# New instruction lists between two checks, dummy products on TensorE, and a weight ring of 19 places instead of 16

## The chip, the cores and the metric

One core of a Trainium2 chip. The time is that of one execution on the device, in microseconds (us), the median over several executions. PE is TensorE (DVE VectorE, ACT ScalarE, POOL GpSimd, SP the engine that issues most DMAs here). An instruction list is what one engine executes in order; engines meet only through semaphores.

## The reference, cut to what matters

```python
x = query                                             # 2 x 2048 x 256, float32
n = layernorm(x)
# 16 heads of 16; 32 learned patterns as keys and values
A = sparsemax(scale * (n @ Wq + bq) @ keys.T)         # per token and head over 32 patterns
x = x + layernorm((A @ values) @ Wo + bo)
n = layernorm(x)
# 16 slots attend to all tokens of a batch (softmax over the tokens)
o = slot_query + mha(slot_query, n, n)
# slot e goes through expert e of 16: 256 -> 1024 -> 256
h = layernorm(o) * g + b
o = o + (silu(h @ W1[e] + b1[e]) * silu(h @ Wg[e] + bg[e])) @ W2[e] + b2[e]
# every token attends to its batch's 16 slots, 16 heads
x = x + layernorm(mha(n, o, o))
```

Sparsemax needs, per token and head, a threshold tau such that max(z - tau, 0) adds up to 1.

## The kernel before

**Groups.** The 4096 tokens are worked on in 8 groups (NG) of 4 tiles of 128 tokens; groups 0 to 3 are batch 0, 4 to 7 batch 1. The residual stream x stays in SBUF (4 MB), as do the transposed second norms ynT (in `arena`, 4 MB): the slot scores read them once early, the last attention again at the end.

**Sparsemax, group i.** ACT normalizes (`norm_y`), PE transposes (`turn_y`) and makes scores into two PSUM banks (`scores_of`), ACT copies them to `scr` (`put_scores`), DVE takes the eight largest of each row of 32 with 16 MAX8 per tile (`sort_top`, L1551) and from their running sums a first tau (`threshold`). POOL subtracts it into `d` in two halves (`subtract`, L556), ACT clamps the halves at zero (`clamp`, L690), DVE marks and adds up (`count`, L1578 and L1579) and makes the final threshold `tauf` (`settle`, L1606). POOL takes it off the stored scores (`lower`, L548), and ACT's `signs` (L699) counts what is positive. After each batch a `check(b)` compares the two counts and, if a row needs it, repairs; it ends with the copy of a flag (L1652), which releases the batch's heads.

**Heads, tile n.** `turn_a` (4 transposes, L1019), `take_a` (ACT), `mix` with block-diagonal values that POOL makes (`values`, L539; semaphore bd_ready), `take_h`, `project` (L1038, L1040), `take_o` (ACT, L721). Then per group: `output_statistics` (DVE), `roots(1)` (POOL), `norm_o` (ACT, L662), `join` (DVE adds it to x, L1677, and takes statistics), `roots(2)`, `second_norm` (ACT), `turn_norm` (PE, L1066), `put_norm` (ACT, writes ynT), `slot_scores` (PE, L1075), `put_slot_scores`.

**The order between the checks.** While DVE does batch 1's sparsemax (groups 4 to 7), PE does batch 0's heads (groups 0 to 3) beside batch 1's scores. All four engines have these parts interleaved by lists written out by hand: on PE the `heads_of(g, steps)` calls with scores and norms between them, on ACT some 90 calls from `take_a(0)` on, on DVE and POOL the loops `for i in range(GB, NG)`. After the second check come batch 1's heads, and beside them the slot softmax and `to_slots` (short products in four steps for each batch, L1116 to L1136).

**Experts.** Weights are 48 loads of 1 MB (W1 and Wg of expert e, W2 of expert e-1, in turns). They go through a ring of R = 16 places of 8 KB per partition, in regions that are free by then (`slots_of`). SP's list issues load n with `fetch(n)`: the first 16 at written-out points between other waits, and from n = R on each when load n - R has been used (up_ps or down_ps). Per expert PE runs `grow` (two products of 512 columns for each of four column strips, L1306), `turn_up` (L1315), `sum_down` of the expert before (L1324) and `shrink` (L1336), with short DVE and ACT steps between. x lies in four of the places: `spill(g)` stores a finished group of x to the output tensor, `unused(j)` waits for two groups' stores and reads before a place of x is loaded, and `restore(j)` (L469) reads a group back when the last weights of its place have been used.

**Last attention.** Two small products each for keys and values (L1357), folds (L1365, L1371), and then per group `scores(j)` (L1388), softmax on DVE, ACT and POOL, `turn_prob` (L1399), `outputs` (L1412), a layernorm, the addition of x and the store.

Of the kernel before, what the change touches and what calls it, by code (L numbers as in the profile page):

```python
# [5 lines left out]
ALU = mybir.AluOpType  # L6
# [28 lines left out]
def build(nc, A, out):  # L35
    with ExitStack() as ctx:
# [3 lines left out]
        def sem(name):  # L40
# [7 lines left out]
        ynT = arena[:, 0:8192].rearrange("p (b c l) -> p b c l", b=NB, c=C)  # L48
# [11 lines left out]
        slots_of = ([home(xflat, 0), home(arena_late, 0), home(arena_late, 1), home(xflat, 1), home(scr1, 0), home(scr1, 1),  # L60
                     home(scr1, 2), home(xflat, 2), home(scr1, 3), heads[:, :], home(arena_late, 2), home(xflat, 3),
                     home(work, 2), home(work, 0), home(work, 1), home(work, 3)])
# [214 lines left out]
        back = [sem(f"back{q}") for q in range(2)]  # L277
        turned = sem("turned")
# [78 lines left out]
        def _(sp):  # L357
# [83 lines left out]
            sp.wait_ge(o_ps, 2 * KT)  # L441
            fetch(9)
# [3 lines left out]
            fetch(10)  # L446
            spill(7)
            unused(3)
            fetch(11)
            sp.wait_ge(g_ps, KT // 2 + KT // 4)  # L450
            fetch(12)
# [8 lines left out]
            def restore(j):  # L460
                if j >= 2:
                    sp.wait_ge(back[j % 2], 16 * (j // 2))
                last = max(n for n in range(3 * NE) if slots_of[n % R] is slots_of[(0, 3, 7, 11)[j // 2]])
                e, k = loads[last]
# [6 lines left out]
            for j in range(NG):  # L471
                restore(j)
# [10 lines left out]
        def _(pool):  # L483
# [96 lines left out]
            for i in range(GB, NG):  # L580
# [76 lines left out]
        def _(act):  # L657
# [28 lines left out]
            def clamp(i):  # L686
                for u in range(2):
# [48 lines left out]
            def put_norm(g):  # L736
                b, at = g // GB, (g % GB) * GT
                act.wait_ge(ynT_ps, g + 1)
                for c in range(C):
                    act.activation(ynT[:, b, c, at:at + GT], bT[c][:, :], ACT.Copy, bias=1.0).then_inc(ynT_sb, 1)  # L740
# [62 lines left out]
            take_a(1)  # L803
            take_h(0)
            clamp(4)
# [3 lines left out]
            put_scores(5, 1, range(2, 3))  # L809
            norm_y(6, tiles=range(2))  # L810
            put_scores(5, 1, range(3, TG))
            take_a(3)
            norm_y(6, tiles=range(2, TG))
# [4 lines left out]
            put_yT(6)  # L818
            take_o(3)
            put_scores(6, 1, range(1))  # L820
            signs(4, 1)
            put_scores(6, 1, range(1, 2))

            take_a(4)
            take_a(5)
            take_h(4)
            clamp(5)
            take_a(6)
            take_h(5)
            take_o(4)  # L830
            put_scores(6, 1, range(2, 3))
            norm_y(7, tiles=range(2))
            put_scores(6, 1, range(3, TG))
            take_a(7)
            take_h(6)
            take_o(5)
            norm_o(0)
            take_h(7)
            take_o(6)
            norm_y(7, tiles=range(2, TG))  # L840
            take_o(7)
            put_yT(7)
            second_norm(0)
            put_scores(7, 1, range(1))
            put_norm(0)
            signs(5, 1)
            put_scores(7, 1, range(1, 2))

            take_a(8)
            take_a(9)  # L850
            take_h(8)
            clamp(6)
            take_a(10)
            take_h(9)
            take_o(8)
            put_slot_scores(0)
            put_scores(7, 1, range(2, 3))
# [1176 lines left out]
```

## Time and profile before

| | us |
|---|---|
| median of 3 executions | 520.99 |
| lowest and highest | 520.46, 526.11 |
| the profiled execution's own time | 524.08 |
| its span, first to last instruction | 522.1 |
| PE busy (share) | 402.4 (77%) |
| DVE busy | 307.9 (59%) |
| ACT busy | 232.6 (45%) |
| POOL busy | 154.1 (30%) |

The profiled execution lasted 2.0 us more than its span. Times in rows are microseconds from the span's start. PEclk is the granted TensorE clock as a share of 2.4 GHz (0.5 is 1.2 GHz). Busy matmul times are modelled ends, so two may overlap; an f32 product is issued as two instructions.

### The profile page before, as it was taken

The page shows a single profiled execution, that of the slowest core. Times are in us where ns is not written, and L with a number is a line of the kernel's source. Part 1 is how long each engine was busy: PE and PEld are TensorE (multiplying, and loading weights), DVE is VectorE, ACT ScalarE, POOL GpSimd, SP SyncE. Part 2 cuts the span into 40 slices and gives each one's busy share as a digit, 9 for nine tenths or more (in the row PEclk, how much of TensorE's full clock was granted, in tenths as well). Part 3 has the DMA queues.
Part 4 walks back from the last instruction along what each step waited for, and adds up shares of the span by engine and source line. Part 5 has one row for each costly group of instructions (what it writes and reads, how often), then busy time and mean ns, then how long its engine had stood idle before and what let it go on. Part 6 is the DMA issues. An engine that isn't in the chain of part 4 may idle for free.

```text
span 522.1 us, 6829 instructions
## 1 busy us (share of the span) xinstructions
PE 402.4 (77%) x2023; PEld 251.6 (48%) x2023; DVE 307.9 (59%) x1176; ACT 232.6 (45%) x422; POOL 154.1 (30%) x253
## 2 busy tenths in 40 slices
PE   3868655869959583958999897599865669999981
PEld 3523222335434342534777666234322227888871
DVE  4699999978786837246522625323312213778994
ACT  2336765745848457547654744000000001237675
POOL 3115465656463452112320210100000000144454
PEclk9997788769989879879999999779989895999996
DMA  5291101101010315245322571579999996201223
GB/s 153 88 332 48 30 12 41 40 1 41 1 41 1 96 56 201 75 146 177 122 81 82 171 272 26 216 266 401 388 398 393 391 374 210 81 1 40 72 85 126
DMA packets 42301, 75.38 MB, mean 144 GB/s; under 512 B 1686, under 2 KB 36124, under 8 KB 38172
## 3 DMA queue, kind: packets, MB, share of 16 engines
q1 hardware_dynamic: 41208, 73.76, 40.3%
q10 hardware_dynamic: 1060, 1.22, 0.8%
q8 instruction: 16, 0.26, 0.2%
q14 instruction: 17, 0.14, 0.1%
HBM read 66.58 MB, written 8.39 MB: 144 GB/s over the span
## 4 chain that ended last, share of the span: by engine, by line
PE 52%; DVE 19%; ACT 8%; DMA 5%; SPq 5%; issue 5%; POOL 4%; DVEq 1%; POOLq 0%; ACTq 0%
PE bank L1075 6%; PE bank L1412 5%; PE bank L1388 5%; SPq L396 5%; PE bank L1104 4%; PE bank L1306 4%; PE bank L1040 4%; DVE top L1551 4%; PE bank L1007 3%; PE bank L1029 3%; DMA arena<-in_L_ffn_e_W_dram 3%; PE bank L1019 2%; DVE stats L1476 2%; DMA work<-in_L_ffn_e_Wg_dram 2%; PE bank L1066 2%
## 5 line engine op out<-in xcount | busy, mean ns | idle before, releaser
L1007 PE MATMUL bank<-Wz,yT 128*128 128x512 f32 x128 | 71.9, 714 | 26.0 <-DVE top L1551 23.4
L1007 PEld LDWEIGHTS bank<-Wz,yT 128*128 128x128 f32 x128 | 28.7, 233 | 61.7 <-issue 49.9
L1551 DVE MAX8 top<-bank 128x8 f32<-128x32 f32 x512 | 51.7, 178 | 6.7 <-ACT scr L683 3.9
L941 ACT ACTIVATE d<-d 128x32 f32<-128x32 f32 x16 | 3.7, 229 | 104.6 <-DVE d L1897 104.6
L526 POOL TENSOR_SCALAR veps<-mv 128x4 f32<-128x4 f32 x24 | 6.7, 278 | 119.4 <-DVE mv L1479 88.8
L1040 PE MATMUL bank<-aWo,hoT 128*128 128x256 f32 x128 | 37.0, 413 | 3.5 <-DVE arena L1665 3.5
L631 POOL TENSOR_TENSOR work<-work 128x512 f32<-128x512 f32 x16 | 16.6, 1060 | 70.1 <-DVE work L1962 70.1
L662 ACT ACTIVATE arena<-arena,shift,rstd 128x256 f32<-128x256 f32 x64 | 33.5, 596 | 2.6 <-POOL shift L646 2.6
L1075 PE MATMUL bank<-arena,Wd 128*128 128x512 f32 x64 | 32.1, 647 | 1.2 <-ACT arena L740 1.2
L1665 DVE TENSOR_TENSOR arena<-bank,Wz 128x256 f32<-128x256 f32 x16 | 6.7, 418 | 43.8 <-PE bank L1040 43.8
L1886 DVE TENSOR_TENSOR d<-bank,slotT 128x4 f32 (+1 forms) x16 | 2.6, 165 | 50.0 <-PE bank L1324 50.0
L1104 PE MATMUL bank<-d,work 128*128 128x256 f32 x128 | 30.2, 381 | 0.5 <-ACT d L768 0.5
L1412 PE MATMUL bank<-scr,work 128*128 128x256 f32 x128 | 29.1, 381 | 1.6 <-ACT work L954 1.6
L1388 PE MATMUL bank<-scr,arena 128*128 128x256 f32 x128 | 29.0, 381 | 0.0
L1040 PEld LDWEIGHTS bank<-aWo,hoT 128*128 128x128 f32 x128 | 22.4, 194 | 13.7 <-issue 9.9
L1029 PE MATMUL bank<-heads 128*64 128x256 f32 x128 | 22.3, 427 | 6.1 <-ACT hoT L713 4.5
L1412 PEld LDWEIGHTS bank<-scr,work 128*128 128x128 f32 x128 | 24.2, 190 | 5.3 <-ACT work L954 2.1
L529 POOL TENSOR_TENSOR rstd<-veps,mhalf 128x4 f32<-128x4 f32 x24 | 26.0, 1083 | 2.0
L707 ACT ACTIVATE heads<-bank 128x512 f32<-128x512 f32 x32 | 18.6, 593 | 17.6 <-PE bank L1019 17.6
L1388 PEld LDWEIGHTS bank<-scr,arena 128*128 128x128 f32 x128 | 24.0, 192 | 3.3 <-DVE work L1949 0.2
L1104 PEld LDWEIGHTS bank<-d,work 128*128 128x128 f32 x128 | 24.1, 196 | 3.0 <-ACT d L768 1.0
L1306 PE MATMUL bank<-x,top 128*32 128x512 f32 x64 | 20.2, 764 | 6.2 <-DMA scr<-in_L_ffn_e_Wg_dram 3.5
(255 smaller groups left out, 872.9 us busy)
## 6 DMA issues: line engine op xcount, KB each, us to landing
x<-in_L_ffn_e_W_dram SPq DMA_DIRECT2D x9, 1024.0 KB, 10.9
scr<-in_L_ffn_e_W_dram SPq DMA_DIRECT2D x8, 1024.0 KB, 13.3
work<-in_L_ffn_e_W_dram SPq DMA_DIRECT2D x8, 1024.0 KB, 14.6
arena<-in_L_ffn_e_W_dram SPq DMA_DIRECT2D x5, 1024.0 KB, 7.6
xin<-in_L_attn_query_dram SPq DMA_DIRECT2D x8, 512.0 KB, 4.1
x<-in_L_attn_query_dram SPq DMA_DIRECT2D x1, 4096.0 KB, 16.6
out_dram<-x SPq DMA_DIRECT2D x8, 512.0 KB, 3.4
arena<-in_L_ffn_e_Wg_dram SPq DMA_DIRECT2D x4, 1024.0 KB, 10.4
```

The costliest lines, as they stand in the source:

```text
L396: sp.dma_start(dst, src).then_inc(e_in[n % R], 16)
L529: pool.tensor_tensor(rstd[:, k, :], veps[:, k, :], mhalf[:, :], ALU.pow).then_inc(root[k], 1)
L662: return act.activation(dst, src, ACT.Identity, bias=shift[:, k, t:t + 1], scale=rstd[:, k, t:t + 1])
L1007: mm = pe.matmul(bZ[t % 2][:, :], yT[:, c, t * P:(t + 1) * P], Wz[:, c, :], start=(c == 0), stop=(c == C - 1))
L1029: mm = pe.matmul(psH[64 * a:64 * a + 64, :], bdh[:, n % TG, :], quarter[:, :, a, :], start=True, stop=True)
L1040: mm = pe.matmul(psO, hoT[:, n % 2, m, :], aWo[:, m, :], start=(m == 0 and n >= KT), stop=(m == 1))
L1075: mm = pe.matmul(bT[m][:, :], Wd[:, c, m * P:(m + 1) * P], ynT[:, b, c, gb * GT:(gb + 1) * GT], start=(c == 0), stop=(c == C - 1))
L1104: mm = pe.matmul((bZ[0] if n < 8 else bank[7])[:, c * 2 * P:(c + 1) * 2 * P], yn[:, kt, c::C], pT[:, n % 2, u * 2 * P:(u + 1) * 2 * P], st ...
L1306: mm = pe.matmul(bank[q][32 * k:32 * k + 32, :], hcol[:, q, c, :], pair[g][:, c * FF + half * 512:c * FF + (half + 1) * 512], start=(c == ...
L1388: mm = pe.matmul(ps, ynT[:, b, c, at:at + P], Wc[:, b, c, :], start=(c == 0), stop=(c == C - 1))
L1412: mm = pe.matmul(ps, cpT[:, u, (v * 2 + m) * P:(v * 2 + m + 1) * P], Vc[:, b, m, :], start=(m == 0), stop=(m == 1))
L1551: mx = v.max(top[:, h * TG + t, :], bZ[t % 2][:, h * NS:(h + 1) * NS])
```

## The change

The diff has four parts.

1. *Lists between the checks.* ACT's calls from `take_a(0)` to `take_o(15)` are in a new order: clamps are split in halves with copies of heads between them, `norm_o(g)` stands whole and early, `signs` of groups 5 and 6 stand later. PE's `heads_of` pieces are cut elsewhere; the first scores of group 7 stand before `turn_norm(0)`, `turn_norm(1)` and `slot_scores(1)` go inside the heads of group 3. POOL makes the next group's first values between `roots(1)` and `roots(2)`. On DVE `count` adds up first and marks after; for group 7 it adds up in two halves, each behind one half of the clamp; `group_maximum(0)` goes behind `threshold`.
2. *Dummy products* (`keep_clock(bank, times)`): each is one bf16 product of 128 x 128 with 512 columns from the constant `chain` into a bank that nobody reads. Nine before `turn_p(12)`; 5, 4, 3, 15 and 4 before and behind the steps of `to_slots(1, ...)`; 4, 3 and 2 around the last expert's `shrink` and `sum_down`.
3. *Norms to DRAM.* ynT is laid out by group. `send_away(g)` stores groups 2 to 7 (0.5 MB each) after `put_norm(g)`, `left(k)` waits for a pair's stores and slot scores, and `fetch_back(k)` reads a pair back after the last weights of its place. `scores(j)` waits for it from group 2 on.
4. *A ring of 19 places*: the three regions of these pairs are places 5, 10 and 15. The early fetches are 19, in the same written-out places of SP's list, and refills start with load 19.

```diff
+            def send_away(g):
+                k = g // 2 - 1
+                sp.wait_ge(ynT_sb, 2 * (g + 1))
+                sp.dma_start(away[k, :, (g % 2) * 1024:(g % 2 + 1) * 1024], arena[:, 1024 * g:1024 * (g + 1)])\
+                    .then_inc(gone[k], 16)
+
+            def left(k):
+                sp.wait_ge(gone[k], 32)
+                sp.wait_ge(s_ps, 2 * (2 * k + 4))
...
             fetch(4)
+            send_away(2)
+            send_away(3)
+            left(0)
+            fetch(5)
             sp.wait_ge(a_ps, KT + 8)
-            fetch(5)
+            fetch(6)
             spill(4)
             sp.wait_ge(a_ps, KT + 12)
-            fetch(6)
+            fetch(7)
+            send_away(4)
             spill(5)
             unused(2)
-            fetch(7)
+            fetch(8)
+            send_away(5)
             sp.wait_ge(a_ps, 2 * KT)
-            fetch(8)
+            fetch(9)
+            left(1)
+            fetch(10)
...
+            fetch(14)
+            send_away(7)
+            left(2)
+            fetch(15)
             sp.wait_ge(pT_ps, KT)
-            fetch(13)
-            fetch(14)
+            fetch(16)
+            fetch(17)
             sp.wait_ge(g_ps, KT)
-            fetch(15)
+            fetch(18)
...
+            fetch_back(0)
+            restore(0)
+            restore(1)
+            fetch_back(1)
+            restore(2)
+            restore(3)
+            fetch_back(2)
+            for j in range(4, NG):
                 restore(j)
```

PE's list, and POOL's and DVE's loops:

```diff
-            heads_of(1, range(3, TG + 2))
+            heads_of(1, range(3, 4))
             turn_y(7)
+            heads_of(1, range(4, TG + 2))
+
+            heads_of(2, range(2))
+            scores_of(7, range(2))
             turn_norm(0)
-            scores_of(7, range(2))
+            heads_of(2, range(2, 3))
             slot_scores(0)
-
-            heads_of(2, range(3))
             scores_of(7, range(2, TG))
             heads_of(2, range(3, TG + 2))
+
+            heads_of(3, range(3))
             turn_norm(1)
+            heads_of(3, range(3, 4))
             slot_scores(1)
-
-            heads_of(3)
+            heads_of(3, range(4, TG + 2))
...
                     roots(1, g - 1)
+                if i < NG - 1:
+                    values(g + 1, range(2))
+                if g > 0:
                     roots(2, g - 1)
                 if i < NG - 1:
                     lower(i, 1)
-                    values(g + 1, range(2))
...
+                if last:
+                    for u in range(2):
+                        v.wait_ge(relued, i * 2 + (u + 1))
+                        v.tensor_reduce(exc[:, u * HR // 2:(u + 1) * HR // 2], d3[:, u * NH // 2:(u + 1) * NH // 2, :, :],
+                                        AX_X, ALU.add).then_inc(newton, 1)
+                else:
+                    v.wait_ge(relued, i * 2 + 2)
+                    v.tensor_reduce(exc[:, :], d3, AX_X, ALU.add).then_inc(newton, 1)
```

ACT's list, the part of groups 5 and 6 (new order):

```python
            clamp(5, range(1))
            take_o(3)
            take_a(4)
            clamp(5, range(1, 2))
            take_a(5)
            take_h(4)
            take_a(6)
            take_h(5)
            norm_y(7, tiles=range(2))
            take_o(4)
            norm_o(0)
            put_scores(6, 1, range(2, TG))
            take_a(7)
            norm_y(7, tiles=range(2, TG))
            ...
            take_o(12)

            signs(6, 1)
            take_a(15)
            take_h(14)
            take_o(13)
            clamp(7)
            mark(7)
            put_slot_scores(1)
            norm_o(2)
            take_h(15)
            take_o(14)
            take_o(15)
            signs(7, 1)
```

The dummy products:

```diff
+            def keep_clock(bk, times):
+
+                idle = chain[:, :, :].rearrange("p r k -> p (r k)")
+                for _ in range(times):
+                    pe.matmul(bank[bk][:, :], idle[:, 0:P], idle, start=True, stop=True)
...
             pe.wait_ge(dve_part, PREP + MS)
-            for step in range(4):
+            pe.wait_ge(hbias, 1)
+            for step, times in enumerate((5, 4, 3, 15)):
+                keep_clock(1, times)
                 to_slots(1, step)
+            keep_clock(1, 4)
...
+                if e == NE - 1:
+                    keep_clock(1, 4)
                 shrink(e)
+            keep_clock(1, 3)
             sum_down(NE - 1)
+            keep_clock(1, 2)
```

## Rows read from the trace of the kernel before

**Rows 1.** Windows by stage: length; busy time (instructions) by engine; PEclk, DMA share, GB/s

```profile
108.37:209.94 101.57, 76.70 (x296) 42.30 (x296) 74.83 (x317) 63.88 (x119) 50.09 (x59) 0.87 0.16 56
209.94:327.20 117.26, 104.49 (x514) 74.55 (x514) 49.44 (x153) 65.38 (x126) 21.14 (x55) 0.96 0.39 131
341.26:427.03 85.77, 62.69 (x560) 26.68 (x561) 23.09 (x72) 3.44 (x15) 2.46 (x13) 0.93 1.02 382
427.03:445.06 18.03, 16.86 (x93) 11.90 (x93) 5.63 (x21) 1.51 (x2) 0.00 (x0) 0.53 0.76 239
445.06:520.50 75.44, 64.91 (x333) 56.76 (x331) 59.96 (x139) 42.31 (x81) 33.03 (x52) 0.95 0.19 63
120.00:150.00 30.00, 24.27 (x112) 13.98 (x110) 24.20 (x120) 21.32 (x44) 16.60 (x20) 1.00 0.11 36
```

**Rows 2.** The page's slices of 13 us, DMA busy in tenths

```profile
DMA  5291101101010315245322571579999996201223
```

**Rows 3.** Groups by line, 108 to 210: busy us, mean ns, idle before

```profile
L1007 PE MATMUL bank<-Wz,yT 128*128 128x512 f32 x40 | 19.9, 644 | 0.0
L1551 DVE MAX8 top<-bank 128x8 f32<-128x32 f32 x192 | 19.5, 178 | 5.0 <-ACT scr L683 3.9 <-issue 1.1
...
L1579 DVE TENSOR_REDUCE exc<-d 128x64 f32<-128x2048 f32 x4 | 9.1, 2278 | 8.1 <-ACT d L690 8.1
...
L699 ACT ACTIVATE above<-scr,tiny 128x2048 bf16<-128x2048 f32 x4 | 8.0, 2000 | 0.0
```

**Rows 4.** Timeline of ACT, norm_o of group 0

```profile
142.05 2.06 ACT L662 ACTIVATE arena<-arena,shift,rstd 128x256 f32<-128x256 f32 x4
```

**Rows 5.** Timeline of POOL, subtraction of group 7

```profile
184.48 3.78 POOL L556 TENSOR_TENSOR d<-scr,tau 128x1024 f32<-128x1024 f32 x2 [0.71 <-DVE tau L1565]
```

**Rows 6.** Timeline of DVE, between the checks: start, duration, instruction, idle before

```profile
144.14 1.23 DVE L1677 TENSOR_TENSOR x<-x,arena 128x1024 f32<-128x1024 f32 x1 [3.08 <-ACT arena L662]
...
177.22 0.23 DVE L1606 TENSOR_TENSOR tauf<-tau,rcnt 128x64 f32<-128x64 f32 x1
...
194.21 2.29 DVE L1579 TENSOR_REDUCE exc<-d 128x64 f32<-128x2048 f32 x1 [8.14 <-ACT d L690]
...
209.94 0.15 DVE L1652 COPY flag<-moved 128x1 f32<-128x1 f32 x1 [2.66 <-issue]
```

**Rows 7.** Timeline of PE, turn_norm(0) and slot_scores(1)

```profile
151.55 1.89 PE L1066 MATMUL bank<-ident,work 128*128 128x128 f32 x8 [4.50 <-ACT work L662]
...
183.47 6.60 PE L1075 MATMUL bank<-arena,Wd 128*128 128x512 f32 x8 [1.18 <-ACT arena L740]
```

**Rows 8.** Timeline of SP's queue: loads 13 and 14, first refill, restores

```profile
323.74 1.00 SPq L396 DMA_DIRECT2D work<-in_L_ffn_e_W_dram  x2
...
341.26 0.38 SPq L396 DMA_DIRECT2D x<-in_L_ffn_e_W_dram  x1
...
422.78 21.85 SPq L469 DMA_DIRECT2D x<-out_dram  x8
```

**Rows 9.** The chain that ended last: start, us, what

```profile
337.57 3.67 PE bank L1306 x16
...
352.25 1.85 PE bank L1306 x16
...
415.73 11.17 DMA work<-in_L_ffn_e_Wg_dram
...
438.10 3.59 PE bank L1357 x16
```

**Rows 10.** Timeline of PE: a bf16 product, and three waits

```profile
126.17 0.26 PE L1038 MATMUL bank<-ab,ones 3*128 3x256 bf16 x1 [0.57 <-ACT arena L721]
...
317.02 1.09 PE L1090 MATMUL bank<-ident,work 128*128 128x128 f32 x8 [2.50 <-ACT work L756]
...
336.10 0.29 PE L1135 MATMUL bank<-ident,yT 16*128 16x16 f32 x1 [3.52 <-DVE yT L1775]
...
434.27 1.93 PE L1336 MATMUL bank<-work,xin 128*32 128x256 f32 x16 [0.28 <-issue]
```

More of the change, by code:

```diff
@@ L277, in build @@
         back = [sem(f"back{q}") for q in range(2)]
+        gone = [sem(f"gone{k}") for k in range(NG // 2 - 1)]
+        home_again = [sem(f"home_again{k}") for k in range(NG // 2 - 1)]
         turned = sem("turned")
@@ L445, in _, with emptied @@
             sp.wait_ge(x_new, NG)
-            fetch(10)
+            fetch(12)
+            send_away(6)
             spill(7)
             unused(3)
-            fetch(11)
+            fetch(13)
             sp.wait_ge(g_ps, KT // 2 + KT // 4)
-            fetch(12)
+            fetch(14)
+            send_away(7)
+            left(2)
+            fetch(15)
             sp.wait_ge(pT_ps, KT)
-            fetch(13)
-            fetch(14)
+            fetch(16)
+            fetch(17)
             sp.wait_ge(g_ps, KT)
-            fetch(15)
+            fetch(18)
             for n in range(R, 3 * NE):
                 fetch(n)
[L460 to L464, printed above, removed]
+            def emptied(place):
+                e, k = loads[max(n for n in range(3 * NE) if n % R == place)]
                 if k < 2:
@@ L468, in restore, with fetch_back @@
                     sp.wait_ge(down_ps, e + 1)
-                sp.dma_start(x[:, j * TG:(j + 1) * TG, :], ot[:, j * TG:(j + 1) * TG, :]).then_inc(back[j % 2], 16)
-            for j in range(NG):
+            def fetch_back(k):
+                emptied(places_y[k])
+                sp.dma_start(arena[:, 2048 * (k + 1):2048 * (k + 2)], away[k, :, :]).then_inc(home_again[k], 16)
+            def restore(j):
+                if j >= 2:
+                    sp.wait_ge(back[j % 2], 16 * (j // 2))
+                emptied(places_x[j // 2])
+                sp.dma_start(x[:, j * TG:(j + 1) * TG, :], ot[:, j * TG:(j + 1) * TG, :]).then_inc(back[j % 2], 16)
+            fetch_back(0)
[6 more added lines that the diff above has]
+            for j in range(4, NG):
                 restore(j)
@@ L684, in put_scores, with clamp @@
                                    bZ[t % 2][:, :].rearrange("p (h s) -> p h s", h=NH), ACT.Copy).then_inc(z_sb, 1)
-            def clamp(i):
-                for u in range(2):
+            def clamp(i, halves=range(2)):
+                for u in halves:
                     half = slice(u * 1024, (u + 1) * 1024)
@@ L803, in _ @@
             take_a(1)
+            clamp(4, range(1))
             take_h(0)
-            clamp(4)
+            clamp(4, range(1, 2))
             take_a(2)
@@ L861, in _ @@
             take_o(9)
-            norm_o(1, range(2, TG))
-            put_scores(7, 1, range(3, TG))
             take_h(11)
             take_o(10)
+            take_a(12)
             take_o(11)
-            second_norm(1)
-            put_norm(1)
-            signs(6, 1)
-            take_a(12)
             take_a(13)
             take_h(12)
-            clamp(7)
-            mark(7)
+            second_norm(1)
             take_a(14)
             take_h(13)
+            put_norm(1)
             take_o(12)
-            put_slot_scores(1)
-            norm_o(2, range(2))
+            signs(6, 1)
             take_a(15)
@@ L883, in _ @@
             take_o(13)
-            norm_o(2, range(2, TG))
+            clamp(7)
+            mark(7)
+            put_slot_scores(1)
+            norm_o(2)
             take_h(15)
@@ L1571, in steps_ahead, with count @@
                 return i * NW if b == 0 else GB * NW + (i - GB) * (NW + 1)
-            def count(i, b, marks):
-                v.wait_ge(relued, i * 2 + 2)
-                if not marks:
-                    v.wait_ge(signed, i)
-                    v.tensor_scalar(above[:, :], d[:, :], 0.0, None, ALU.is_gt).then_inc(newton, 1)
-                v.tensor_reduce(exc[:, :], d3, AX_X, ALU.add).then_inc(newton, 1)
+            def count(i, b, marks, last=False):
+                if last:
[6 more added lines that the diff above has]
+                    v.tensor_reduce(exc[:, :], d3, AX_X, ALU.add).then_inc(newton, 1)
                 if marks:
@@ L1591, in settle @@
             def settle(i, b, marks, last=False):
-                at = steps_ahead(i, b) + (2 if marks else 3)
+                at = steps_ahead(i, b) + (2 if marks and not last else 3)
                 v.wait_ge(newton, at)
@@ L1817, in _ @@
                     output_statistics(g - 1)
-                count(i, 1, i == NG - 1)
+                count(i, 1, i == NG - 1, last=i == NG - 1)
                 if 0 < g < 3:
```

79 lines of the change are left out of this document (40 added, 39 removed).

## The prediction

> **What bounds the kernel now.** I read the windows by stage first [rows 1]. The reader is to see that no one engine carries the whole span. Between the two checks (108.37 to 209.94) PE is busy 76.7 of 101.6 us, DVE 74.8, ACT 63.9: nobody is full, so the stage is a chain that goes round the engines. From 209.94 to 327.2 PE has 104.5 of 117.3 us. In the experts (341.26 to 427.03) the DMA share is 1.02 at 382 GB/s while PE has 62.7 of 85.8: loads bound it. From 445 on PE is the bound again until the last tiles. The page's slice row of DMA [rows 2] shows the same plateau of nines, nine slices long, and next to nothing in most slices ahead of it. So a gain must come from the chain between the checks, from fewer loads left when the experts start, or from PE's clock in the 32 us around the experts, where the grants are low (0.53 in the row of 427.03 to 445.06).
>
> **Between the checks.** I walked the four instruction lists of the new kernel, with this stage's durations: 16 MAX8 per tile 1.6 us (0.178 us each, overlapping a little), one big sum 2.28, one tile of scores on PE 1.7, a sign pass 2.0 plus 0.1 [rows 3], four scaled tiles on ACT 2.06 [rows 4], a subtraction 3.78 in two halves [rows 5]; an instruction starts when its engine is free and its releaser has been done for 0.05 to 0.25 us, as in the trace.
> - Group 4: nothing differs until ACT's clamp. ACT clamps the first half before it copies heads, and DVE adds up before it marks, so tauf comes at 120.3 instead of 120.7.
> - Group 5: the signs of group 4 no longer part the first two score copies of group 6, and take_o(3) stands behind half a clamp. DVE's output statistics end at 133.7 (before: 135.8), POOL's roots at 135.9 (138.9). Now norm_o(0) stands right behind take_o(4), so ACT runs it from 136.0 to 138.1; before, it stood behind a projection that waits for four score products, and ran from 142.05 [rows 4]. DVE idled 3.08 us on it and joined at 144.14 [rows 6]. In the new order DVE finishes its count at 139.0 and joins at once. tauf: 143.5 instead of 148.7, 5.2 earlier.
> - Group 6: PE stood 4.50 us before turn_norm(0), with the scores of group 7 behind it, and the clock fell in the wait (its 8 transposes took 1.89 us) [rows 7]. In the new order the scores of group 7 go first: tiles at 148.7 and 150.4. The output statistics end at 155.0 (163.7), the clamp at 157.8 (165.5), the count at 163.0, norm_o(1) at 160.7, the join at 166.1. tauf: 167.6 instead of 177.4 [rows 6], 9.8 earlier.
> - Group 7: group_maximum(0), 1.2 us, goes behind the threshold. Threshold at 173.9, subtraction done at 178.0 instead of 188.26 [rows 5]: 10.2 earlier.
> - The end: mix(14) needs the values that POOL makes only after that subtraction, and ACT's clamp(7) now stands behind take_h(14) and take_o(13). PE idles some 7 us before it, so I let it run at half clock there, as it did at 183.5 (slot scores 6.60 us [rows 7]). Clamp done at 183.5, mark 185.4, count 187.4, tauf 189, DVE's lowering 191.2, join 194.3 (norm_o(2) at 190.1), signs(7) 194.5, and the check's own 3.8: settled at 199.5 instead of 209.94. Before, the count had idled 8.14 us on the clamp [rows 6], 6 us after the subtraction's end; it is 5.5 in the walk, so this tail gains next to nothing.
>
> I take 10.5 us off. Bounds: 13 off if PE keeps its full clock at the end (slot scores 3.4 instead of 6.6); 4 off if each of the steps that I let run tightly loses 2 us, which is what the seen waits vary by. After the check the same lists run as before, so the later stages only move. POOL's reordered values(g+1) ahead of roots(2) cost nothing: their h_ps is long there.
>
> **Six groups' norms away, ring of 19.** Added: six stores of 0.5 MB between 214 and 312 us, three loads of 1 MB back, and four waits for PE and DMA on SP's queue. What is queued behind these waits on SP are the fetches and the spills, each of which was already held by something near: left(0) lets fetch(5) go at 238 (s_ps of group 3), left(1) at 283, left(2) at 313; send_away(4) holds spill(5) 6 us, and unused(2) behind it came at 269 anyway. The last early loads still go at 323.7 and 327.2 [rows 8] with little in flight before, land by 334, and so all 19 places are full before the first refill. The DMA is at 131 GB/s in that stage [rows 1], so 6 MB more hide. Price without that cover: 0.5 MB at 382 GB/s is 1.4 us each.
> Then the experts. The first refill is issued at 341.26 [rows 8], when grow(0) is done; PE waits for Wg of expert 15, load 45, until 426.9 [rows 9]. With 16 places these are loads 16 to 45, 30 of them in 85.7 us; 2 us are the first one's way, so 2.79 each (1.05 MB at 382 GB/s: 2.74). With 19 places three fewer: 8.4 us. PE could go faster: grow steps stand 4.2 us apart where it has its weights, so 15 experts after the first need 63 us of the 77 that are left; the bound stays DMA. Bounds: 8.2 to 8.6 if all three are in; none if they come late.
> Read-backs: restore(0) is issued at 422.78, behind the last weights [rows 8]; now 1 MB stands before it and 2 MB between the restores. 7 MB from about there at 260 to 390 GB/s are 18 to 27 us. Group 2's norm, first in the queue, lands before 440 where PE wants it at 455 (this trace's times), groups 4 and 6 have 15 us more each. Cost 0; if the cover went, 2.7 us for each MB.
>
> **Dummy products.** One is a bf16 product of 512 columns. The trace has only 256 bf16 columns (0.26 us [rows 10], the next product 0.21 later) and f32 instructions of 512 columns (16 in 1.85 at full clock, four beside each other in the array, so 0.46 for each four [rows 9]). So it lies between 0.21 and 0.46; I take 0.22, because an f32 product is issued as two instructions for the same columns and bf16 as one, and 0.43 at half clock.
> - Nine before turn_p(12): 2.0 us in a wait of 2.50 [rows 10]. Clock there is 1.00 already. 0.
> - 5, 4, 3, 15 and 4 in the slot steps of batch 1: 6.8 us in gaps of 1.0, 0.7, 0.5, 3.5 [rows 10] and 0.8. The overhang is 0.6. They keep the clock: grow(0) took 3.67 us at half and takes 1.85 at full [rows 9], the small transposes 0.3 less. The refill starts at grow(0)'s end, and DMA bounds from there, so the gain goes through once: net 1.5 off. Bounds: 2 off, and 6.8 lost if a dummy takes 0.43 and more.
> - 4, 3 and 2 around the last expert: PE waits there 0.28 [rows 10], 0.54 and 0.35 us, 3.9 us of dummies at half clock, so 2.7 lost. If they lift the clock at once, shrink(15), sum_down, L1357 (3.59 for 16 [rows 9]) and what follows halve: 3.8 gained against 0.8 lost, 3.1 off. I take 0, near the middle.
>
> What the row of the tail shows: PE is busy 16.9 of 18.0 us at a granted 0.53 [rows 1], that is 1.2 GHz most of the time although it hardly rests; it ran instructions of 512, 2, 256 and 32 columns there, and the clock is back at 445 after three groups of 128 and 256. The Trainium skill (TensorE: Matmul & The Clock Gate, Part 1: The HAM clock gate) says that the slow clock is the default and that sustained activity of the engine releases it. By it alone the tail ought to have been fast already, and a few wide products more should make it so: the tail term would be -3.1 instead of 0. This trace does not agree, by 17 us of that row; the rule stays as a rival below.
>
> **The sum.** The profiled execution took 524.08 us, its span 522.1, 2.0 lie around it. -10.5 -8.4 -1.5 + 0 = -20.4: 503.7 for an execution like that one. The median shown is 520.99, 3.1 below it; the same terms on the median give 500.6.
>
> **Rivals.**
> - *The chain between the checks loses its slack.* PE falls to half clock at each wait, not only the last, and norm_o, join and clamp slip 2 us three times: 4.5 off instead of 10.5, 506.6. For it: the clock fell at both norm waits before [rows 7]. Against it: it was 1.00 from 120 to 150 [rows 1], and the new order has fewer waits until the last group.
> - *The wide dummies lift the clock in the tail.* 3.1 off more, and the stage between the checks at its better end by 1: 496.5. Worked out: shrink(15) 0.9, sum_down 0.4, L1357's first half 0.9 and what hangs on it 1.6, less 0.8 of dummies. For it: the clock did come back at 445 once the products were back to back. Against: in the row of 427.03 to 445.06 the engine was nearly as busy, and it did not.
> - *The ring gives nothing.* The three more loads are held on SP (left(2) or a spill late) and still outstanding at 341: 8.4 fewer, 509.0. Against: the three loads issued from 323.7 on take 10 us, so 7 us lie between their landing and the first refill.
> - *Slower: the clock of the whole stage.* PE's products between the checks are 76.7 us at 0.87, or 66.7 us of full clock; the rest of the stage, 24.9, is not PE's. If the new order makes PE's work arrive in pieces, at mean clock c the stage takes 66.7/c + 24.9. It eats the other terms' 10 us at c = 0.77 and makes the kernel 1% slower at 0.73; at 0.70 the stage takes 120 us, 18.6 more, and the kernel 529.7. Against it: the 1.00 above, and less idle PE to pull it down.
>
> **How the numbers follow.** Forecast 0.50; chain without slack 0.22; clock lifted in the tail 0.17; ring nothing 0.07; slower 0.04. The forecast's own range is 497 to 504. For 8 in 10, the first two rivals belong in it with their spread: 494.5 to 508.5, which leaves out the ring's case and the slow one and some of each edge. A change of 1% (5.2 us) is about what a measurement tells from none. All cases but the last are faster by more than 1% (0.96, and I give 0.95); the last is split: 0.03 within 1%, 0.02 slower.
>
> **What would show it.** In the profile after: the second flag near 199.5 and the subtraction of group 7 ending near 178; DVE's idle before its join of group 0 gone; experts from first refill to the wait for Wg of expert 15 in 77 us instead of 85.7, DMA share still 1.0; first grow in 1.9 us; norms back before PE asks, so no wait of L1388 on DMA. It is wrong if PE's waits in the experts vanish (then PE bounds and 8.4 is too much), if a wait for the norms opens a gap between 445 and 500, or if the stage's PE clock is under 0.85.

## The result, and the profile after

The changed kernel takes 499.23 us (median of 4, 496.82 to 501.44), the kernel before 523.55 beside it (median of 4, 520.46 to 527.11). The ratio is 0.9586, interval 0.954 to 0.9632: 4.1% faster, where 3.9% was forecast and 500.6 us. The medians lie 24.3 us apart. The profiled execution took 501.44, its span is 499.4, so 22.7 us less span than before; the stages below are read from this one execution of each kernel.

The windows by stage of the changed kernel, cut at the same events as [rows 1] (flag to flag, flag to first `grow`, first refill to the wait for Wg of expert 15, from there to the first score of the last attention, and the rest):

```profile
109.44:202.16 92.72, 72.63 (x296) 40.44 (x296) 75.64 (x317) 63.22 (x118) 45.18 (x59) 0.88 0.17 62
202.16:331.25 129.09, 118.10 (x579) 81.51 (x579) 53.96 (x169) 66.09 (x128) 22.44 (x61) 0.95 0.55 187
333.23:409.77 76.54, 62.75 (x560) 26.90 (x561) 23.20 (x72) 3.44 (x15) 2.46 (x13) 0.91 1.02 384
409.77:422.39 12.62, 12.04 (x101) 7.29 (x101) 5.18 (x20) 1.51 (x2) 0.00 (x0) 1.00 1.04 365
422.39:498.00 75.61, 64.87 (x333) 56.72 (x332) 60.32 (x141) 42.31 (x81) 33.04 (x52) 0.97 0.32 106
```

The reader is to see four things. The first row has almost the same busy times as before in 8.85 us less. The third has the same DMA share in 9.2 us less. The fourth has a granted clock of 1.00 where it was 0.53. The last carries three more megabytes of read-backs and is as long as before: from the first score to the end of the span it is 77.01 us, before 77.04, and no score product there waited for a DMA.

| stage, us | before | after | difference | term in the sum |
|---|---|---|---|---|
| start to first flag | 108.37 | 109.44 | +1.07 | 0 |
| flag to flag | 101.57 | 92.72 | -8.85 | -10.5 |
| second flag to first grow | 127.63 | 129.09 | +1.46 | +0.3 |
| first grow to first refill | 3.69 | 1.98 | -1.71 | -1.8 |
| refill to wait for load 45 | 85.77 | 76.54 | -9.23 | -8.4 |
| that wait to first score | 18.03 | 12.62 | -5.41 | 0 |
| first score to end | 77.04 | 77.01 | -0.03 | 0 |

The critical chain shows where the new bounds lie. DMA has 4% of it (before 5%), and the dummies (L1189) now stand in it, each four in 0.86 to 0.97 us:

```profile
322.79 0.86 PE bank L1189 x4
...
330.35 0.97 PE bank L1189 x4
331.32 1.90 PE bank L1358 x16
```

The first `grow` takes 1.90 us; its answer in [rows 9] took 3.67.

### The profile page after: what moved, and what is told of

It is laid out like the page before. It is cut to its first block, busy times and chain, and to the rows that moved or that the text cites. A ratio compares the mean times of both kernels' runs of the same rounds, so it can differ in the third digit from the quotient of the medians.

```text
span 499.4 us, 6939 instructions
## 1 busy us (share of the span) xinstructions
PE 403.0 (81%) x2072; PEld 249.7 (50%) x2072; DVE 308.8 (62%) x1177; ACT 232.0 (46%) x422; POOL 149.2 (30%) x253
## 4 chain that ended last, share of the span: by engine, by line
PE 53%; DVE 20%; ACT 8%; issue 5%; SPq 5%; DMA 4%; POOL 3%; DVEq 1%; POOLq 0%; ACTq 0%
PE bank L1469 6%; PE bank L1445 6%; PE bank L1112 5%; PE bank L1078 5%; PE bank L1141 5%; PE bank L1045 4%; DVE top L1608 4%; SPq L403 4%; PE bank L1358 4%; DMA x<-in_L_ffn_e_W_dram 3%; PE bank L1067 3%; DVE exc L1639 2%; DVE stats L1533 2%; PE bank L1057 2%; PE bank L1388 2%
## 5 line engine op out<-in xcount | busy, mean ns | idle before, releaser
L1045 PE MATMUL bank<-Wz,yT 128*128 128x512 f32 x128 | 70.7, 704 | 24.2 <-DVE top L1608 21.6
L1078 PE MATMUL bank<-aWo,hoT 128*128 128x256 f32 x128 | 39.4, 434 | 3.5 <-DVE arena L1727 3.5
L568 POOL TENSOR_SCALAR veps<-mv 128x4 f32<-128x4 f32 x24 | 5.7, 237 | 110.4 <-DVE mv L1536 83.3
L1078 PEld LDWEIGHTS bank<-aWo,hoT 128*128 128x128 f32 x128 | 23.7, 205 | 14.1 <-issue 10.2
L1112 PE MATMUL bank<-arena,Wd 128*128 128x512 f32 x64 | 29.9, 610 | 0.0
L571 POOL TENSOR_TENSOR rstd<-veps,mhalf 128x4 f32<-128x4 f32 x24 | 24.9, 1039 | 2.0
L1358 PE MATMUL bank<-x,top 128*32 128x512 f32 x56 | 17.1, 742 | 7.0 <-DMA arena<-in_L_ffn_e_Wg_dram 3.6
## 6 DMA issues: line engine op xcount, KB each, us to landing
arena<-in_L_ffn_e_W_dram SPq DMA_DIRECT2D x9, 1024.0 KB, 13.8
```

Of the source, the lines that this page charges most:

```text
L571: pool.tensor_tensor(rstd[:, k, :], veps[:, k, :], mhalf[:, :], ALU.pow).then_inc(root[k], 1)
L1045: mm = pe.matmul(bZ[t % 2][:, :], yT[:, c, t * P:(t + 1) * P], Wz[:, c, :], start=(c == 0), stop=(c == C - 1))
L1078: mm = pe.matmul(psO, hoT[:, n % 2, m, :], aWo[:, m, :], start=(m == 0 and n >= KT), stop=(m == 1))
L1112: mm = pe.matmul(bT[m][:, :], Wd[:, c, m * P:(m + 1) * P], ynT[:, g, c, :], start=(c == 0), stop=(c == C - 1))
L1358: mm = pe.matmul(bank[q][32 * k:32 * k + 32, :], hcol[:, q, c, :], pair[g][:, c * FF + half * 512:c * FF + (half + 1) * 512], start=(c == ...
```

## The experiments

Four executions each, compared with the kernel before on the same chip. The stages are read from the profile of one of them, as in the table above; all numbers are us, "changed" is the changed kernel, "experts" is from the first refill to PE's wait for load 45, and "tail" from there to the first score of the last attention. The kernel before had medians of 523.55, 521.35, 521.04 and 522.45 in four measurements, the changed kernel 499.23 and 498.36. So the stages carry the argument and the medians confirm it, and differences of 1 or 2 us in a median say little.

| run | median | flag to flag | flag to grow | to refill | experts | tail |
|---|---|---|---|---|---|---|
| before | 523.55 | 101.57 | 127.63 | 3.69 | 85.77 | 18.03 |
| changed | 499.23 | 92.72 | 129.09 | 1.98 | 76.54 | 12.62 |
| e1 lists only | 511.85 | 90.23 | 128.27 | 3.69 | 85.65 | 15.22 |
| e2 ring only | 514.06 | 101.56 | 132.84 | 3.46 | 76.25 | 15.36 |
| e3 dummies only | 517.75 | 101.76 | 129.85 | 1.99 | 84.05 | 12.60 |
| e4 no dummies | 502.82 | 90.23 | 128.07 | 3.70 | 77.46 | 15.48 |
| e5 no tail dummies | 502.22 | 90.60 | 128.20 | 1.98 | 76.54 | 14.91 |
| e6 values first | 494.70 | 85.62 | 129.38 | 1.98 | 76.02 | 12.61 |
| e7 dummies at the check | 498.68 | 90.87 | 127.93 | 1.99 | 76.25 | 13.48 |
| e8 both | 490.93 | 86.78 | 126.74 | 1.98 | 76.85 | 12.58 |
| e9 changed again | 498.36 | 92.72 | 129.06 | 1.98 | 75.93 | 12.60 |
| e10 no head dummies | 505.12 | 92.73 | 128.95 | 3.69 | 77.39 | 13.75 |
| e11 no ring | 508.40 | 92.74 | 129.10 | 1.99 | 84.37 | 12.61 |

### e1: the lists alone

The kernel before with the new lists of ACT, PE, POOL and DVE; nothing else of the diff.

> The kernel before with the new lists alone (16 places, no dummy products, norms stay). My theory: the parts add up, each in its own stage. The stage between the two checks takes 92 to 94 us instead of 101.6 and everything behind it only moves, so the time is 8 to 10 us under the kernel before (ratio 0.981 to 0.985). Rival: PE's half clock in the first slot scores after the second check gives part of it back in a part of the profiles; then 6 to 7 us.

Measured: 511.85 us (508.87 to 514.29), ratio 0.9815 (0.974 to 0.9891). Flag to flag is 90.23. The lists give 11.3 us in this stage (7.6 to 9.6 expected) and hand on all of it but 0.6. My theory held; the rival's half clock behind the second flag is there, but it was there before too. The tail is 2.8 us shorter although nothing in it was touched. PE entered it at full clock in both profiles: before, the clock fell 1 to 2 us later, here only in the group of 32-column products, 8 us in.

### e2: the ring alone

The parts 3 and 4 of the diff (spill, read-back, 19 places), old lists, no dummies.

> The kernel before with the norms' spill and the ring of 19 alone. My theory: loads bound the experts, so from the first refill to the wait for Wg of expert 15 it takes 76.5 to 77.4 us instead of 85.8, and the rest stays as it was: 8 to 9.5 us under the kernel before (ratio 0.982 to 0.985). Rival for the tail: if the 5.4 us that the changed kernel gained between that wait and the first score of the last attention come from where the last wait falls and not from the dummies, the tail is 12.6 us long here too and the gain is 13 to 14 us; if the dummies make it, the tail stays 18.

Measured: 514.06 us (511.34 to 517.95), ratio 0.9866 (0.9783 to 0.9949). The experts take 76.25, as my theory wants. Neither expectation for the tail held: it is 15.36, between both. And 5.2 us were lost between the second flag and the experts, which I had not expected. PE's timeline shows 3.1 of them; the first two lines stand where the changed kernel has its nine dummies:

```profile
318.73 1.97 PE L1130 MATMUL bank<-ident,work 128*128 128x128 f32 x8 [2.50 <-ACT work L797]
320.53 3.78 PE L1144 MATMUL bank<-d,work 128*128 128x256 f32 x8
...
335.54 1.89 PE L1171 MATMUL bank<-d,hT 128*16 128x256 f32 x4 [0.47 <-DVE hT L1801]
```

The same eight transposes took 1.09 us before, behind the same wait of 2.50 [rows 10], and the product behind them 2.00:

```profile
318.37 2.00 PE L1104 MATMUL bank<-d,work 128*128 128x256 f32 x8 [0.25 <-ACT d L768]
```

The two groups end 2.2 us later for it, and the last line's half clock (1.89 us, before 1.04) costs 0.9. The other 2.1 lie ahead of the wait: behind the second flag the clock came back later than in the profile before. The clock can fall in this wait or not: it fell here, and not in the kernel before, in e1 and in e4, each with the same wait of 2.50.

### e3 and e4: the dummies alone, and none of them

```diff
 e3: the kernel before, plus every keep_clock(...) of the diff
 e4: the changed kernel, less every keep_clock(...)
```

> The kernel before with the dummy products alone. My theory: grow(0) starts at full clock and takes 1.9 us instead of 3.7 (net 2 us earlier for the first refill), and the tail shortens from 18 to 13 us only if the dummies are its cause: 7 us under the kernel before in all (ratio 0.986). Rival (the tail is luck of the last wait): 2 us in all (ratio 0.996), tail 17 to 18.

> The changed kernel without any dummy product. My theory: lists and ring keep 18 us, 2 are lost at the head of the experts; whether the tail is 18 us again (505 to 507 in all) or stays near 13 (501 to 502) tells whether the dummies or the place of the last wait made the tail short.

Measured: e3 517.75 us (515.74 to 519.58), ratio 0.993 (0.9861 to 1.0); e4 502.82 us (502.41 to 503.88), ratio 0.9648 (0.9584 to 0.9712). The tail is 12.60 with the dummies and 15.48 without, so both theories were half right: 2.9 us come from the dummies, and the other 2.5 of the 5.4 from where the clock happened to fall in the profile before (the part on the tail, below, compares them). e3's median is 3.6 us under the kernel before, half of my 7, while the two profiled spans differ by 6.8. In its profile 2.1 us are lost behind the second flag, ahead of the first dummy, where its program is the kernel before's, and e2 lost the same 2.1 there: that is not the edit. What else parts the median from the profile stays open.

### e5: no dummies in the tail

```diff
-                if e == NE - 1:
-                    keep_clock(1, 4)
                 shrink(e)
-            keep_clock(1, 3)
             sum_down(NE - 1)
-            keep_clock(1, 2)
```

> The changed kernel without the nine dummy products around the last expert; the 31 in the slot steps and the nine before them stay. If these nine make the short tail (my theory after the first four runs), the stretch from the wait for Wg of expert 15 to the first score of the last attention takes 15.2 to 15.5 us where PE enters it at full clock and 18 where not, and grow(0) still takes 1.9 us. Rival: the 2.9 us between the runs with and without dummies come from the head's dummies too (a clock that stayed up); then the tail stays 12.6.

Measured: 502.22 us (500.7 to 507.78), ratio 0.97 (0.96 to 0.9799). The tail is 14.91, and `grow(0)` still short: the nine make it. PE's timeline of e5, last expert on:

```profile
413.17 1.07 PE L1388 MATMUL bank<-scr,xin 128*32 128x256 f32 x16 [0.62 <-DMA scr<-in_L_ffn_e_W_dram]
414.78 0.63 PE L1376 MATMUL bank<-sel,y 128*128 128x2 f32 x4 [0.55 <-DVE y L1939]
415.76 1.45 PE L1409 MATMUL bank<-d,Wz 128*128 128x32 f32 x8 [0.35 <-DVE d L1944]
417.03 1.89 PE L1409 MATMUL bank<-d,hoT 128*128 128x32 f32 x8
418.74 2.05 PE L1417 MATMUL bank<-d,above 128*128 128x128 f32 x8
420.58 1.91 PE L1423 MATMUL bank<-aWo,d 128*128 128x256 f32 x4
```

and of the changed kernel:

```profile
415.77 1.07 PE L1388 MATMUL bank<-scr,xin 128*32 128x256 f32 x16
416.77 0.82 PE L1189 MATMUL bank<-chain 128*128 128x512 bf16 x3
417.43 0.59 PE L1376 MATMUL bank<-sel,y 128*128 128x2 f32 x4
417.88 0.59 PE L1189 MATMUL bank<-chain 128*128 128x512 bf16 x2
418.37 1.05 PE L1413 MATMUL bank<-d,Wz 128*128 128x32 f32 x8
419.26 1.06 PE L1413 MATMUL bank<-d,hoT 128*128 128x32 f32 x8
420.45 1.16 PE L1421 MATMUL bank<-d,above 128*128 128x128 f32 x8
421.45 1.03 PE L1427 MATMUL bank<-aWo,d 128*128 128x256 f32 x4
```

Both enter at full clock. Without the dummies it falls within the first group of 32-column products (1.45 us, then 1.89 for the same eight); with them the last three groups run in little more than half the time. The dummies did not lift a fallen clock, they kept a full one. They did two things at once, they filled PE's gaps and they put wide products between narrow ones; which of the two kept the clock, no run separates.

### e6: values first

```diff
+                if g == 3:
+                    values(g, range(2, TG))
                 subtract(i, 1)
-                if g > 0:
+                if 0 < g < 3:
                     values(g, range(2, TG))
```

> The changed kernel with POOL making the second pair of values of group 3 before the last subtraction instead of after it. In the changed kernel PE stands 5.84 us before mix(14) on these values, and ACT's last clamp stands behind it. My theory: that couples the clamp to PE, so the clamp's halves come 5 to 6 us earlier and the stage between the checks is 4 to 6 us shorter (87 to 88.5 us). Rival: the chain then waits for the output norm of group 2 and the lowered signs, which gives only 1 to 2 us.

Measured: 494.7 us (493.63 to 495.17), ratio 0.9529 (0.948 to 0.9578). Flag to flag is 85.62, 7.1 less than in the changed kernel's profile and better than I had expected. Of these, 5.0 are the swap: from the subtraction's end to the flag it is 15.5 us, in the changed kernel, e1 and e4 20.5. The other 2.1 lie ahead of the subtraction, where a wait of PE differed (see the part on the stage between the checks). The median is 3.7 us under e9's and 4.5 under the changed kernel's. PE's timeline of the changed kernel, with the wait, and DVE's, with its idle time for the clamp:

```profile
175.60 0.60 PE L1057 MATMUL bank<-ident,arena 128*128 128x128 f32 x4
182.04 1.12 PE L1067 MATMUL bank<-heads 128*64 128x256 f32 x4 [5.84 <-issue]
183.09 0.39 PE L1076 MATMUL bank<-ab,ones 3*128 3x256 bf16 x1
183.41 2.08 PE L1078 MATMUL bank<-aWo,hoT 128*128 128x256 f32 x4
185.28 4.38 PE L1112 MATMUL bank<-arena,Wd 128*128 128x512 f32 x8
```

```profile
186.88 2.35 DVE L1635 TENSOR_REDUCE exc<-d 128x32 f32<-128x1024 f32 x2 [6.21 <-ACT d L734]
```

and the same places of e6:

```profile
173.95 0.65 PE L1069 MATMUL bank<-heads 128*64 128x256 f32 x4 [0.29 <-issue]
...
175.93 3.60 PE L1114 MATMUL bank<-arena,Wd 128*128 128x512 f32 x8
```

```profile
178.62 1.22 DVE L1637 TENSOR_REDUCE exc<-d 128x32 f32<-128x1024 f32 x1 [0.49 <-ACT d L736]
180.26 1.22 DVE L1637 TENSOR_REDUCE exc<-d 128x32 f32<-128x1024 f32 x1 [0.42 <-ACT d L736]
```

PE's wait is gone and with it the half clock behind it, and DVE's idle time before the last sums falls from 6.21 to 0.9. The trace puts PE's wait down to "issue"; the run shows that it was POOL's values, queued behind a subtraction that needs group 7's threshold. POOL's timeline, of the changed kernel and of e6, has the two in either order:

```profile
177.91 3.78 POOL L598 TENSOR_TENSOR d<-scr,tau 128x1024 f32<-128x1024 f32 x2 [2.67 <-DVE tau L1622]
181.65 0.55 POOL L581 TENSOR_TENSOR heads<-vrep,jmask 128x64 f32<-128x64 f32 x2
```

```profile
172.65 2.00 POOL L581 TENSOR_TENSOR heads<-vrep,jmask 128x64 f32<-128x64 f32 x2
175.36 3.78 POOL L598 TENSOR_TENSOR d<-scr,tau 128x1024 f32<-128x1024 f32 x2 [0.71 <-DVE tau L1624]
```

The values took 0.55 us behind the subtraction, and PE began at 182.04.

### e7 and e8: dummies in the wait for the check

```diff
+            pe.wait_ge(a_sb, KT)
+            keep_clock(4, 26)
             for n in range(KT, 2 * KT + 2):
                 heads_step(n, KT, 2 * KT)
```

> The changed kernel with 26 dummy products more, on PE before the heads of batch 1, in its wait for the second check (6.8 us idle in the profile, half clock behind it until about 209). If the clock bounds the first heads of batch 1, from the second flag to grow(0) it takes 1.5 to 3 us less than 129.1; rival: the wait for psO, the norms and the statistics bounds there and nothing changes.

> Values first and the 26 dummies together. If both hold as expected, the stage between the checks is 87 to 88.5 us, what follows 1.5 to 3 us shorter, and the whole 6 to 8 us under the changed kernel. If PE then still idles before the second check, the dummies are still hidden; if not, they add up to 5.7 us and the gain is lost.

Measured: e7 498.68 us (496.89 to 499.34), ratio 0.9591 (0.9538 to 0.9645), not to be told from the changed kernel. Flag to `grow` is 127.93, 1.2 less than in the changed kernel's profile but only 0.3 less than in e5's, so e7 alone decides nothing; its dummies ended 1.1 us after the flag. e8, with e6's edit too: 490.93 us (489.7 to 493.15), ratio 0.9445 (0.9396 to 0.9495), 126.74 us from flag to `grow`, 2.4 less than the changed kernel and 2.6 less than e6. It is the best of all: its slowest execution is under e6's fastest (493.63). In e8 the 26 dummies ran while DVE was at the check, and the heads behind it ran at full clock:

```profile
189.41 6.89 PE L1191 MATMUL bank<-chain 128*128 128x512 bf16 x26
196.28 0.66 PE L1059 MATMUL bank<-ident,scr 128*128 128x128 f32 x4
196.77 1.18 PE L1106 MATMUL bank<-ident,work 128*128 128x128 f32 x8
```

In the changed kernel the two groups behind the dummies took 1.12 and 1.91 us. The dummies end 0.2 us after the flag at 196.07, so a few less would do.

### e9 to e11: the changed kernel again, no head dummies, no ring

```diff
 e10:
-            for step, times in enumerate((5, 4, 3, 15)):
-                keep_clock(1, times)
+            for step in range(4):
                 to_slots(1, step)
-            keep_clock(1, 4)
 e11: the changed kernel with the 16 places and the loads of the kernel before, norms not spilled
```

> The changed kernel itself once more, as the measure for the two runs beside it and for how far its stages vary between profiles. Theory: 497 to 501; between the checks 90 to 93 us, from the second flag to grow(0) 127.5 to 130, experts 76 to 77.5, tail 12.6 to 13.5; what varies is where the half clock falls, not the work.

> The changed kernel without the 31 dummies in the slot steps (the nine before turn_p(12) and the nine of the tail stay). Theory: grow(0) at half clock, 3.7 us to the first refill instead of 2.0, about 0.3 us earlier start: 1.5 to 2 us slower than the changed kernel. If the refill's start did not bound the experts, no difference.

> The changed kernel with 16 places and the norms kept in SBUF; lists and all dummies as changed. Theory: experts 84 to 86 us from the first refill to the wait for Wg of expert 15, everything else as in the changed kernel: 8 to 9.5 us slower. Rival: the spilled norms cost something before or after (DMA beside the heads, read-backs beside the last attention), then the other stages are shorter here.

Measured: e9 498.36 us (497.2 to 501.24), e10 505.12 us (502.32 to 505.59), e11 508.4 us (504.59 to 509.81). Against e9, e11 loses 10.0 us in the median and 8.4 in the experts, and every other stage is within 0.2: the spill and the read-backs cost nothing. The rival fell. e10 loses 6.8 us in the median where I expected 1.5 to 2, and 4.0 in the profile: 1.7 to the refill, 1.5 in the experts, 1.2 in the tail. The tail's part is not shown to be the head dummies' work: PE entered it at half clock (its last `grow` took 3.56 us), and so it did in e7, which has them all (3.31 us, tail 13.48). SP's timeline of e10 shows where the experts' part comes from:

```profile
335.05 0.38 SPq L403 DMA_DIRECT2D x<-in_L_ffn_e_W_dram  x1
...
340.65 0.33 SPq L403 DMA_DIRECT2D arena<-in_L_ffn_e_Wg_dram  x1
```

and the same of e9:

```profile
333.69 0.38 SPq L403 DMA_DIRECT2D x<-in_L_ffn_e_W_dram  x1
...
337.12 0.33 SPq L403 DMA_DIRECT2D arena<-in_L_ffn_e_Wg_dram  x1
```

At half clock `grow(1)` is late too, and the third refill comes 5.6 us after the first instead of 3.4. By the prediction's 2.74 us for each, the first two refills are 5.5 us of DMA work, an estimate by which the queue ran nearly dry. The 2.8 us between the median's loss and the profile's are the choice of the execution: e9's profile is of its slowest, 501.24, which is 2.9 over its median, e10's (505.13) of its median one. e4, without a single dummy, has a median of 502.82, under e10's; so 6.8 us is not the price of the 31.

## Why the prediction was right, point by point

**Between the checks: right in mechanism, one step too hopeful.** The walk's milestones count from the first flag. tauf of group 5: 35.1 forecast, 34.5 measured; the join of group 0 follows its count with no idle time, as written. tauf of group 6: 59.2 forecast, 61.3 measured. The failing step is "tiles at 148.7 and 150.4" for the scores of group 7. PE's timeline of the changed kernel:

```profile
128.21 1.04 PE L1057 MATMUL bank<-ident,arena 128*128 128x128 f32 x8
131.80 0.75 PE L1067 MATMUL bank<-heads 128*64 128x256 f32 x4 [2.55 <-ACT heads L751]
...
135.14 2.08 PE L1078 MATMUL bank<-aWo,hoT 128*128 128x256 f32 x4
137.00 4.62 PE L1045 MATMUL bank<-Wz,yT 128*128 128x512 f32 x8
```

take_a(4) stands behind half a clamp and take_o(3), PE waited 2.55 us for it, and the clock fell for the next 7 us (a projection of 2.08 us against 1.13 at full clock). The scores came 2.4 us later than walked. In e1 and e4 the same lists take 90.23, under the 91.1 walked; e1's PE timeline at the same place:

```profile
130.67 0.65 PE L1026 MATMUL bank<-heads 128*64 128x256 f32 x4 [1.44 <-ACT heads L709]
...
134.39 3.60 PE L1004 MATMUL bank<-Wz,yT 128*128 128x512 f32 x8
```

In e1 the granted clock from 134 to 142 was 1.00 (in e4 from 132 to 140 too), in the changed kernel's profile 0.68. What goes with it is the wait: 2.55 or 2.56 us in the four profiles that took 92.7 (the changed kernel, e9, e10, e11), 0.25 to 1.53 in the four that took 90.2 to 90.9 (e1, e4, e5, e7). Why PE comes to this place earlier in some executions stays open. So -10.5 lies between the two ways that this stage runs, -8.9 and -11.3. The rival "the chain loses its slack" was the right mechanism at a fraction of its size.

**The end of this stage** was forecast to gain next to nothing because mix(14) waits for values behind the subtraction: subtraction's end to flag 21.5 us forecast, 20.5 measured, 21.7 before. e6 shows that this wait was worth 5.0 us (15.5). The prediction named the wait and left it.

**Ring: right.** 8.4 us forecast. The four profiles with 16 places take 85.77, 85.65, 84.05 and 84.37 us in the experts, mean 84.96; the nine with 19 places 75.93 to 77.46, mean 76.58: 8.4. Against e9, e11 shows 8.4 as well. DMA share stayed 1.02. Spill and read-back at nothing: shown by e11 and by the last stage, 76.9 to 77.4 in every run. One reading of the prediction was off without harm: DMA's row of slices [rows 2] has six nines in its plateau, not nine slices.

**Head dummies: right in what they do, and too low.** 0.22 us each was right (nine in 2.1 us), and grow(0) gave its 1.7. In the profile the refill comes only 0.25 us sooner after the second flag, because slot_scores(3), long before any dummy, is already 1.3 us late against the flag (half clock behind the check). The step that was too low is "the gain goes through once". In four profiles without head dummies (before, e1, e4, e10) the third refill came 5.5 to 5.6 us after the first; these are the longest in the experts of their kind, 85.77 and 85.65 with 16 places, 77.46 and 77.39 with 19. In the other nine it came 3.4 us after, and the experts took 84.05 and 84.37, or 75.93 to 76.85. So the dummies give another 1.1 to 1.5 us in the experts, and of the 9.2 there the ring's part is 7.9 to 8.4. e2 is among the nine though it has no dummies: its clock came back inside grow(0).

**Tail: wrong, by its clock.** "I take 0, near the middle" measured -5.4, outside my bound of -3.1. The step had priced the dummies at half clock, since the tail of the kernel before ran so by its mean of 0.53. That mean hid where the clock fell. PE came to the tail of the kernel before at full clock and lost it inside the last `grow`:

```profile
426.00:428.00 2.00, 0.97 (x12) 0.45 (x16) 0.00 (x0) 0.00 (x0) 0.00 (x0) 1.00 1.09 347
428.00:430.00 2.00, 2.00 (x15) 0.63 (x6) 0.00 (x0) 0.00 (x0) 0.00 (x0) 0.57 1.10 347
```

The last `grow` of the kernel before, of e2 and of e4:

```profile
427.03 2.45 PE L1306 MATMUL bank<-work,top 128*32 128x512 f32 x16 [3.54 <-DMA work<-in_L_ffn_e_Wg_dram]
...
422.13 1.92 PE L1346 MATMUL bank<-scr,top 128*32 128x512 f32 x16 [3.42 <-DMA scr<-in_L_ffn_e_Wg_dram]
...
407.50 3.35 PE L1347 MATMUL bank<-scr,top 128*32 128x512 f32 x16 [1.21 <-DMA scr<-in_L_ffn_e_Wg_dram]
```

e2 waited nearly as long and kept its clock until the 32-column products. e4 entered at half clock and had it back at the end of this `grow`, and so had e7 and e10. The four other profiles without dummies in the tail (e1, e2, e4, e5) all lost the clock at the 32-column products and took 14.9 to 15.5 us, so the 18.03 of before was an unlucky draw worth some 2.5 us, and the dummies' part is 2.3 to 2.9. The eight profiles with them never lost it: 12.6 us, and 13.5 and 13.8 where they entered at half clock. The rival with the lifted clock (3.1; its own terms add up to 3.0) had nearly the size of the dummies' part, for the wrong reason: where the dummies ran, the clock was already full, and they kept it. The Trainium skill says (TensorE: Matmul & The Clock Gate, Part 1: The HAM clock gate) that sustained activity releases the slow clock. e4, e7 and e10 agree: the clock came back inside their last `grow` (3.35, 3.31 and 3.56 us, against 1.92 at full clock). The tail of the kernel before does not: PE was busy 16.9 of 18.0 us and had half the clock from 430 to 444. And e5 shows that such a stretch can lose a full one.

**The nine dummies** were priced at 0 since the clock there was full. Of the four profiles without them (before, e1, e2, e4) the clock fell in one, e2; there transposes and products took 2.7 us more and ended 2.2 later.

The errors have opposite signs: tail 5.4 better and experts 0.8; the stage between the checks 1.7 worse, the stretch behind it 1.2, the start 1.1, the refill 0.1. So the sum, 20.4, came within 2.3 us of the 22.7 measured. That it is so near is in part luck: the largest error is how the tail of the one profiled execution before ran. The slower rival, half clock over the whole stage, did not come: 0.88 was granted, 0.87 before.

## What to carry to other kernels

A ring of prefetched weights in front of a stage that DMA bounds is worth its bytes over the rate, place by place, even when live data must be stored and read back for it, as long as the queue is idle on both sides. Where a stage is a chain through four engines, look for the instruction that an engine's list puts behind something it does not need: here one swap on the least busy engine gave 5 us of its stage and some 4 in the median, beside the 23 of the whole change. Cheap wide products in a wait are insurance for the clock of what follows, and are to be sized to end with the wait. And read the clock over time, not as a mean over a stage: 0.53 looked like a stage that runs slow, and was a clock that fell 1 to 2 us into it.

## What the runs showed of the hardware that I had not expected

- The clock's fall depends on more than the program. The kernel before took 518.3 to 524.4 us in the seven executions beside e1, at a mean granted clock between 0.884 and 0.916, lowest in the three slowest. A wait of 2.50 us cost nothing in the kernel before, in e1 and in e4, and 2.2 us in e2. The last `grow` kept the full clock behind a wait of 3.42 us in e2 and of 3.50 in e11, and lost it behind one of 3.54 in the kernel before.
- In e5's tail, where products of 2 to 256 columns stand between gaps of 0.3 to 0.6 us, PE went from 2.4 to 1.2 GHz in the first 32-column group; nine products of 512 columns put into these gaps held 2.4 GHz in eight profiles. Whether the filled gaps or the width held it was not tried.
